# Attention stage of a hybrid kernel: the fronts of all four sequences moved ahead of the attention loop, split parts of all eight units kept in DRAM, rotary halves swapped by DMA

## The reference

```python
cq  = gelu(x @ wq + bq)            # 64 latent channels
q_c = cq @ wqc + bqc               # 128 "content" channels
q_r = x @ wqr + bqr                # 128 "rotary" channels
ckv = gelu(x @ wkv + bkv); k_c = ckv @ wkc + bkc; k_r = x @ wkr + bkr
v   = (ckv @ wv + bv)              # 16 heads of 16
q_r, k_r = rope(q_r), rope(k_r)    # t * cos + concat(-t2, t1) * sin
q, k = gelu(concat(q_c, q_r)), gelu(concat(k_c, k_r))   # exact in float32
out = softmax(causal(q k^T / 4)) v
x   = x + (out @ wo + bo)          # x was layer-normed at the input of q, k, v
```

## Time and profile before

| | |
|---|---|
| runs | 5124.07, 5140.43, 5151.45 us; median 5140.43 |
| the profiled execution | 5133.93 us, its span 5132.2 us |
| attention stage in it | from about 3717 to 4726 us |
| ahead of its loop | 3717 to 3854 us |
| the loop | 3854 to about 4718 us, then the last output products |
| mean granted PE clock | 0.867 of 2.4 GHz |

### The profile page before, as it was taken

One profiled execution on the slowest core, in us unless ns is written; L12 is line 12 of the kernel. 1 busy time (PEld: TensorE's weight loads), 2 busy tenths in 40 slices (PEclk: granted clock), 3 DMA queues, 4 the chain that ended last, 5 costly groups with the idle time before them and its releaser, 6 DMA issues.

```text
span 5132.2 us, 49428 instructions
## 1 busy us (share of the span) xinstructions
PE 3978.6 (78%) x15218; PEld 2283.6 (44%) x15218; DVE 2808.6 (55%) x4916; ACT 2304.2 (45%) x4166; POOL 2539.4 (49%) x2184
## 2 busy tenths in 40 slices
PE   6888878769948777996778699948937777788892
PEld 2333333357715455773333356645712323233571
DVE  6999999841156663114888822255244545454422
ACT  5566656321157663113555333332525555555241
POOL 6999999722222333114889644423552424222256
PEclk8999999869969887997888799969957878889896
DMA  5666666512110001223555411150532404221145
GB/s 151 160 156 161 161 160 155 149 42 96 64 50 17 33 25 57 82 78 103 150 153 144 137 43 45 45 158 20 149 87 52 79 19 70 38 39 39 51 130 133
DMA packets 310841, 472.53 MB, mean 92 GB/s; under 512 B 34634, under 2 KB 167734, under 8 KB 310506
## 3 DMA queue, kind: packets, MB, share of 16 engines
q1 hardware_dynamic: 277152, 388.87, 28.9%
q0 software_dynamic: 29184, 76.12, 5.3%
q10 hardware_dynamic: 4224, 4.19, 0.2%
HBM read 375.26 MB, written 97.49 MB: 92 GB/s over the span
## 4 chain that ended last, share of the span: by engine, by line
PE 39%; DVE 6%; POOL 6%; ACT 5%; issue 5%; DMA 3%; SPq 0%; another core or an unknown queue 0%; DVEq 0%; POOLq 0%; ACTq 0%
PE s_gate_up L2305 7%; PE s_result_sum L2321 4%; PE s_out_sum L3632 3%; PE s_hidden_sum L1745 3%; PE s_result_sum L1756 3%; PE s_scores_T L3616 2%; POOL s_h L435 2%; PE s_shared L2961 2%; DVE s_maxima L3272 2%; PE s_scores L3577 2%; PE s_shared L2971 1%; PE s_transposed L2295 1%; POOL s_gathered L1047 1%; POOL s_h L444 1%; DMA s_bc<-s_bc_rows 1%
## 5 line engine op out<-in xcount | busy, mean ns | idle before, releaser
L435 POOL TENSOR_TENSOR s_h<-s_dtu,s_bc 128x1024 f32<-128x1024 f32 x384 | 904.2, 2363 | 73.0 <-PE s_y_sum L477 54.1
L477 PE MATMUL s_y_sum<-s_h,identity 128*128 128x512 f32 x1536 | 770.3, 639 | 160.5 <-POOL s_h L444 151.5
L402 ACT ACTIVATE s_decay<-s_dt,s_A 128x512 f32<-128x512 f32 x768 | 498.4, 682 | 330.3 <-DVE s_h L377 323.3
L477 PEld LDWEIGHTS s_y_sum<-s_h,identity 128*128 128x128 f32 x1536 | 295.0, 202 | 599.2 <-issue 302.4
L3430 ACT ACTIVATE s_weights_T<-s_scores_T 128x1024 f32<-128x1024 f32 (+3 forms) x384 | 302.9, 810 | 369.9 <-PE s_scores_T L3616 364.7
L3272 DVE TENSOR_REDUCE s_maxima<-s_scores 128x1 f32<-128x512 f32 (+3 forms) x438 | 279.0, 659 | 318.0 <-PE s_scores L3580 223.3
L2305 PE MATMUL s_gate_up<-s_w_gate_up,s_rowsT 128*128 x1184 | 420.8, 488 | 3.2 <-issue 2.5
L444 POOL TENSOR_TENSOR s_h<-s_h,s_bc 128x512 f32<-128x512 f32 x288 | 367.0, 1275 | 23.4 <-DVE s_h L370 15.5
L2364 DVE TENSOR_TENSOR s_mid<-s_act,s_gate_up 128x128 f32<-128x128 f32 (+1 forms) x228 | 92.9, 408 | 455.4 <-ACT s_act L2337 433.1
L3492 POOL TENSOR_SCALAR_AFFINE_SELECT s_weights_T<-s_weights_T 128x256 f32<-128x256 f32 x256 | 104.3, 412 | 458.6 <-ACT s_weights_T L3430 457.3
L370 DVE TENSOR_TENSOR_SCAN s_decay<-s_decay,s_carry,s_h 128x512 f32<-128x512 f32 x240 | 303.4, 1278 | 24.3 <-POOL s_clip_flag L2633 13.9
(11 more groups left out here) (525 smaller groups left out, 7989.9 us busy)
## 6 DMA issues: line engine op xcount, KB each, us to landing
s_bc<-s_bc_rows SPq DMA_DIRECT2D x384, 512.0 KB, 4.9
sorted_results<-s_result SPq DMA_DIRECT2D x160, 128.0 KB
s_w_inter<-in_L_ffn_experts_inter SPq DMA_DIRECT2D x16, 1024.0 KB
s_w_exp_out<-in_L_ffn_experts_out SPq DMA_DIRECT2D x16, 1024.0 KB
s_queries<-parts_of_q SPq DMA_DIRECT2D x96, 128.0 KB
s_keys<-parts_of_k SPq DMA_DIRECT2D x96, 128.0 KB
results_by_token<-zeros SPq DMA_DIRECT2D x16, 512.0 KB, 6.1
s_pair<-results_by_token SPq DMA_DIRECT2D x16, 512.0 KB, 6.8
```

Source lines behind the costliest of these rows:

```text
L402: S.e.activation(self.decay[:, (2 * g + d) % 4, :], dt[q // self.passes % 2][:, at, :], ACT.Exp, scale=A[:, at, g % ns:g % ns + 1]).then_i ...
L435: G.e.tensor_tensor(self.h[r][:], dtu[q // self.passes % 2][:, at:at + 2, :], mid(self.bc[r][:, 0, :], 2), ALU.mult).then_inc(*self.fed.up())
L477: made = T.e.matmul(self.y[:, d, :], ident[:], self.h[r][:, d, :], start=False, stop=g % ns == ns - 1)
```

## The change

1. A new function `head` runs ahead of the loop, for every engine, the combine, the front and the split of **all four** sequences as a pipeline with a period of 21 ticks for each sequence, and in it unit 0's maxima and values. `program` now starts at unit 0 and has only `project`, `bias`, `values`, `highest` and `maxima` as sides.
2. `stage` writes the parts of each unit to its own place in DRAM (8 units x 3 parts for q and for k), through a ring of three SBUF tiles. In the head SP stacks units 0 and 1; in the loop it stacks only.
3. The rotary halves are swapped by two DMAs issued by ACT; cos, sin and the sum move from POOL to DVE. Content and rotary tiles have SBUF of their own.
4. A split has two ACT casts (three before) and two subtractions, the second of which writes the third bf16 part. The rotary q tile is subtracted on DVE, the other three on POOL.
5. The combine's ring has four tiles (two before). The front's SBUF is shared with the loop's weights, outputs and the like; DVE and ACT wait at the loop's start until the last three parts tiles have been written to DRAM (`head_is_over`). All eight PSUM banks serve the head. `latent` is kept for each sequence.
6. Ticks of the loop: `FIRST` 14 to 10, `OUT` respaced.

```diff
-    combine = Combine(K, M, X, 2, 1)
+    combine = Combine(K, H, X, 4, 1)
+    parts = [H.sb(f"parts{i}", [P, 3, L], BF16) for i in range(3)]
+    dram = [K.nc.dram_tensor(f"parts_of_{n}", [NB * DT, 3, P, L], BF16, kind="Internal").ap() for n in "qk"]
+    PERIOD, HEAD_MAX, HEAD_VALUES = 21, 62, (112, 114)
+    GATHER, SUM, STATS, FACTORS = (-4, -2, 0, 2, 5, 8, 10, 12), (4, 6, 8, 9, 11, 13, 15, 18), (10, 19), (13, 20)
+    NORM, TURN, TURNED = ((14, 15), (21, 22)), ((16, 17), (24, 25)), ((17, 18), (25, 26))
+    LATENT, LATENT_MADE, CONTENT, CONTENT_MADE = (20, 31), (21, 32), ((23, 24), (34, 35)), ((25, 26), (35, 36))
+    ROTATE, ROTATED, CROSS, ROTARY_MADE = ((28, 30), (36, 38)), ((29, 31), (37, 39)), (35, 43), (39, 47)
+    SPLIT = (((36, 38, 40, 42), (38, 40, 42, 45)), ((41, 44, 45, 49), (48, 50, 52, 54)))
-    FIRST = 14
+    FIRST = 10
+    def head(**side):
+        work = [("setup", 0)]
+        for b in range(NB):
+            work += [(n, b) for n in ("gathers", "sums", "stats", "factors", "norm", "turn", "turned_rows", "latents",
+                                      "content", "rotate", "cross", "rotary")]
+            work += [("split", (b, ct, j)) for ct in range(DT) for j in range(2)]
+        work += [("highest", (0, 0)), ("maxima", (0, 0, False)), ("maxima", (0, 1, False)), ("values", 0)]
     def program(main, **side):
-        for u in range(-3, n_units + 1):
+        for u in range(n_units + 1):
-            if 0 <= u + 2 < n_units:
-                work += [("front", u + 2), ("split", (u + 2, 0)), ("split", (u + 2, 1))]
...
+        def stage(b, ct, j):
+            i = 4 * b + 2 * ct + j
+            Q.wait_ge(*split_done[ct][j].at(b))
+            Q.wait_ge(*staged[i % 3].at(i // 3 - 1))
+            Q.e.dma_start(dram[j][DT * b + ct].rearrange("a c t -> c a t"), parts[i % 3][:]).then_inc(*staged[i % 3].dma())
+        for b in range(NB):
+            if b == NB - 1:
+                stack_max(0, 0)
+            for ct in range(DT):
+                for j in range(2):
+                    stage(b, ct, j)
+                if b == 0:
+                    for a in range(2):
+                        stack(ct, a)
+        for u in range(n_units):
+            if 0 < u < n_units - 1:
+                stack(u + 1, 1)
+            stack_max(u, 1)
+            if u + 2 < n_units:
+                stack(u + 2, 0)
+            if u + 1 < n_units:
+                stack_max(u + 1, 0)
...
+    def rests(E, v):
+        b, ct, j = v
+        to = parts[(4 * b + 2 * ct + j) % 3]
+        yield PERIOD * b + SPLIT[ct][j][1]
+        E.wait_ge(*cast0[ct][j].at(b))
+        E.e.tensor_tensor(act[ct][j][:], act[ct][j][:], to[:, 0, :], ALU.subtract).then_inc(*rest[ct][j].up())
+        yield PERIOD * b + SPLIT[ct][j][3]
+        E.wait_ge(*cast1[ct][j].at(b))
+        E.e.tensor_tensor(to[:, 2, :], act[ct][j][:], to[:, 1, :], ALU.subtract).then_inc(*split_done[ct][j].up())
+    def head_is_over(E):
+        for i in range(2 * n_units - 3, 2 * n_units):
+            E.wait_ge(*staged[i % 3].at(i // 3))
...
+        def cross(b):
+            for j in range(2):
+                yield PERIOD * b + CROSS[j]
+                V.wait_ge(*swapped.at(2 * b + j))
+                for i, (to, table) in enumerate(((act[1][j], cos), (crossed, sin))):
+                    V.e.tensor_tensor(to[:], to[:], table[:], ALU.mult).then_inc(*v_step.up())
+                V.e.tensor_tensor(act[1][j][:], act[1][j][:], crossed[:], ALU.add).then_inc(*rope_added.up())
...
+                for half in range(2):
+                    S.e.dma_start(crossed[half * DC:(half + 1) * DC, :],
+                                  act[1][j][(1 - half) * DC:(2 - half) * DC, :]).then_inc(*swapped.dma())
-                for half in range(2):
-                    made = S.e.activation(crossed[half * DC:(half + 1) * DC, :],
-                                          straight[(1 - half) * DC:(2 - half) * DC, :], ACT.Copy)
```

More of the change, by code:

```diff
@@ L3112, in projects @@
         return range(u // DT * PAIRS - 2, u // DT * PAIRS) if u > 0 else ()
[L3114 to L3117 removed]
     B = Banks()
[L3120 removed]
+    B.of["bv"], B.of["max", 0, 0] = 7, 4
+    for i in range(2):
+        B.of["values", 0, i] = 3 + i
+    for a, n in ((0, PER), (1, EARLY)):
+        for i in range(n):
+            B.of["scores", 0, a, i] = 1 + i % 2
+    for u in range(n_units + 1):
@@ L3320, in main @@
                 beside(2 * s + 1)
-        program(main, setup=setup, combine=sums, front=front, maxima=maxima, highest=highest, project=project)
+        head(setup=setup, sums=sums, stats=stats, cross=cross, split=split, maxima=maxima, highest=highest)
+        head_is_over(V)
+        program(main, maxima=maxima, highest=highest, project=project)
+    def rests(E, v):
+        b, ct, j = v
+        to = parts[(4 * b + 2 * ct + j) % 3]
[8 more added lines that the diff above has]
+            E.wait_ge(*staged[i % 3].at(i // 3))
     def scalar():
@@ L3332, in setup, with norm @@
             made.then_inc(*bv_here.up())
+        def norm(b):
+            for i, c in enumerate(range(b * CPB, (b + 1) * CPB)):
+                for t in range(0, TPC, 2):
+                    yield PERIOD * b + NORM[i][t // 2]
+                    if t == 0:
+                        S.wait_ge(*ln.made.at(c))
+                        S.wait_ge(*turned.at(DT * c - 1))
+                    for a in (t, t + 1):
+                        made = S.e.activation(xn[:, a, :], X[:, TPC * c + a, :], ACT.Identity,
+                                              bias=ln.addend[:, 0, a:a + 1], scale=ln.factor[:, 0, a:a + 1])
+                made.then_inc(*ln.used.up())
@@ L3493, in main, with take @@
                 beside(2 * s + 1)
-        program(main, combine=sums, front=front, rope=rope, split=split, bias=bias)
+        head(gathers=gathers, factors=factors, split=split)
+        program(main, bias=bias)
     def tensor():
         T.wait_ge(*prepared.at(0))
-        free = [turned.at(-1)] * 3
-        ob_free = [turned.at(-1)]
-        def take(name, until):
-            f = B.of[name]
+        free = [turned.at(-1)] * len(bank)
+        def take(f, until):
             T.wait_ge(*free[f])
@@ L3660, in main @@
                     product(n - 2)
-        program(main, setup=setup, values=values, front=front, rotate=rotate, maxima=maxima, highest=highest, project=project)
+        head(setup=setup, turn=turn, latents=latents, content=content, rotate=rotate, maxima=maxima, highest=highest,
+             values=values)
+        program(main, values=values, maxima=maxima, highest=highest, project=project)
     sync()
```

440 lines of the change are left out of this document (199 added, 241 removed).

## The result

The kernel after takes 5057.44 us (median of 4 runs, 5052.76 to 5065.05) against 5135.31 us for the kernel before: a ratio of 0.9847, 95% interval 0.9816 to 0.9879. It is 78 us faster. The forecast was 4937 us, 198 us faster, with a range that ended at 5050. The direction was right; the size was less than half, and both terms of the sum were off by about the same 60 us.

A forecast was written before the change was run, and what follows sets the result against it. No engine was full, so the prediction counted only the attention stage, its loop units lengthened by fronts: 5133.9 - 256 (loop) + 59 (longer head) = 4937 us. The forecast went from 4890 to 5000, the range from 4860 to 5050.

The forecast's parts named there:

- Part 1: Loop: without fronts, units 0 to 6 fall from 114.6 to 78 us, a gain of 256 us (bounds 172 and 312).
- At full clock its 74.0 us of PE work at 0.88 would be 65, and with the same 12 us of idle time the unit would last 77: Loop: unit 6 before, which had no front, scaled to full clock to give the length of every unit.
- the window of 86.3 us: Loop before: last group of unit 5 to last of unit 6, taken as holding all of a unit without a front.
- the forecast's 78: Loop: length in us assumed for each unit from 0 to 6 without fronts, between 70 and 90.
- the rival of units of 90 us: Loop: stack copies come late, units last 90 us, total 5021 us; chance 0.10.
- the rival of the clock: Loop: the clock stays at 1.2 GHz, units last 126 us, total 5273 us, slower; chance 0.03.
- Part 2: Head: it grows, so the loop starts at 3913, 59 us later than before (bounds 25 and 125).
- Up to the gathers of the fourth sequence POOL runs in its written order, and I take it as the bound: Head: POOL's gathers, subtractions and norm factors set the pace, with the last gather ending at 3845.
- Staging behind stacking: Head: stagings queue behind stack copies on SP and hold ACT's casts and POOL's subtractions; 10 us (0 to 24).
- beside it: Head's tail of 48 us: unit 0's maxima, values and highest run alongside, costing up to 20 us if cover is short.
- Contention of POOL and DVE: Head: DVE operations with two SBUF inputs and POOL's tensor operations wait for each other; 10 us on POOL (0 to 60).
- The rival in which DVE's 70 us stand in series with POOL's work: Head: the shared port sets the pace, total 4997 us; chance 0.12.

The follow-up runs named there:

- b1_nostack: The kernel after without the stacking copies of units 2 to 7, which then use queries and keys of units 0 and 1; ratio 0.985 to the kernel before.
- a4_noprod: The kernel after with the output projection (turning the rows, product, addition into the residual) left out; units of 79.4 us, ratio 0.973 to the kernel before.
- a3_both: The kernel after with each tile's statistics halves together on DVE and units 0 and 1 stacked behind all four stagings of their sequence; 5016.36 us, ratio 0.978.
- d2_shrunk: a3_both with unit 0's score maxima in the head taken over the first 32 keys only, without mask there; head 209.8 us, ratio 0.977.
- c1_copies: The kernel after with the rotary halves swapped by two ACT copies, as in the kernel before, instead of two DMAs; ratio 0.983 to the kernel before.

## Why the prediction was right and wrong

**Right.** The seat of the time: fronts out of the loop raise its clock (0.84 to 0.92) and take PE, ACT and POOL work from it. The last 58 us stayed. No table load is left in the loop: ACT loads the exponential's table once, at 3971.53. The stack copies in the loop cost nothing (b1_nostack). The loop does not stay at 1.2 GHz.

**Part 1, 256 us forecast, 196 measured.** The step that failed is "At full clock its 74.0 us of PE work at 0.88 would be 65, and with the same 12 us of idle time the unit would last 77". No unit runs at full clock. By the windows above the clock is 0.94 in unit 1 and 0.89 in unit 5, and PE's busy time follows it: 72.44 x 0.94 = 68.1 and 76.87 x 0.89 = 68.4, with 14 us of idle time in both. So scaling by the clock was sound; the clock put in was not: the one window of the earlier trace rows that has a unit's products and values stood at 0.88. In the mean of units 1 to 6 PE is busy for 74.15 us at 0.92 and idle for 14.3. Of the 11.5 us between this unit of 88.5 and the 77, about 6 are the clock (74 against 68), 3 are work (68 against 65), and 2 idle time. Of the work 1.2 us are eight small products of the values: a unit from 1 to 5 has 486 matmuls, while the window of 86.3 us, which was said to have "all of it", has 478. The rest of the 3 us was not traced. The bare 86.3 us, which stood in the earlier trace rows, would have been the better number.

Over the forecast's 78, six units of 88.5 us are 63 us too long, and unit 0, which has no output product, lies some 3 below it: that is the 60. The output products are not what was left out. Every unit from 1 on carries two, but so did unit 6 of before, from which the 77 was taken. That a4_noprod comes out at 79.4, beside the forecast's 78, is luck: it lacks 9.1 us of work and waits that the forecast had in it. The rival of units of 90 us had the length nearly right and the reason wrong, since the stack copies cost nothing; the rival of the clock had the reason, but far too much of it. Each unit still has a stretch at low clock, as unit 6 had before: in unit 2 it lies between 4144 and 4160, at 0.68. Such stretches did not go with the fronts, and what brings them is not shown.

**Part 2, 59 us forecast, 118 measured.** The step that failed is "Up to the gathers of the fourth sequence POOL runs in its written order, and I take it as the bound". The pace was set by order. Measured from the stage's first load, the forecast head was 195.6 us (3913 - 3717.4) and the real one 254.5, beyond the 250 at which the prediction called itself wrong. Of these 59 us, 31.5 went with the two edits of order (a3_both): DVE's aggregation behind the rotary products of the sequence before, which the forecast did not have, and SP's stacks ahead of stagings ("Staging behind stacking", priced at 10). Another 13.2 went with unit 0's maxima (d2_shrunk), which the forecast had "beside it", at up to 20 us if the cover is short; it was short. What is left, 14.2 us, splits at the last gather: it comes in d2_shrunk at 138.3 instead of 127.6 us, and from there to the loop are 71.5 instead of 68 us. The cause of those 11 us at the gathers is not shown. DVE's additions wait 37.3 us for gathers to land, in 15 waits, where it was 13.6 us before, while stagings and stacks keep the DMA share at 0.98 for 60 us; no run took the DMA traffic out of the head, so this stays an argument.

**Contention of POOL and DVE** was priced at 10 us on POOL. Groups by line of the kernel after in the head, POOL's subtractions and the DVE operations that meet them:

```profile
L1064 DVE SCALAR_TENSOR_TENSOR residual<-s_gathered,pick_weight,residual 128x256 f32<-128x256 f32 x64 | 37.5, 586 | 38.5 <-DMA s_gathered<-sorted_results,pick_row 37.3
...
L3368 POOL TENSOR_TENSOR s_act1k<-s_act1k,s_parts 128x1024 f32<-128x1024 f32 x4 | 9.5, 2386 | 14.1 <-ACT s_parts L3452 14.1
...
L3371 DVE TENSOR_TENSOR s_parts<-s_act1q,s_parts 128x1024 bf16<-128x1024 f32 x4 | 6.8, 1692 | 3.9 <-ACT s_parts L3455 3.9
```

The 24 subtractions of POOL took 55 us, 4 more than 24 times 2.13. On DVE the additions took 586 ns in the mean instead of 490 undisturbed, 6 us in all: four of the 64, each beside a subtraction of POOL, took 1.5 to 3.0 us, and the others 0.45 to 0.52. The four subtractions took 1692 ns in the mean instead of 1210, all of it in one that met POOL's and took 3.11 us. The lock of the earlier trace rows is there, and costs some 4 us on POOL and 11 on DVE; how much of it lies on the way to the loop was not tested. The rival in which DVE's 70 us stand in series with POOL's work did not come. The Trainium skill (SBUF — State Buffer, Who interferes with whom) calls it an exclusive lock, and says that a DVE instruction with two SBUF inputs contends with a GpSimd instruction that reads SBUF. The trace agrees for tensor operations by the durations above, and shows next to none of it for gathers, which last 1045 ns here beside the additions and 1018 before.

## What to carry to other kernels

In a software pipeline whose order is written out by tick, a generator that yields between its parts can put a short instruction, on which the next stage hangs, behind another stage's wait; look in the profile for the waits upstream of the idle engine, not for the busiest engine. Two such chains side by side hide each other: one edit gained 14.7 us, the other 1.0, both 31.5, so an edit that does nothing alone is worth keeping until its neighbour is cut. And price a stretch of work by the whole length of a measured stretch with the same contents; if it is scaled to another clock, let it be a clock that such a stretch has had, not the full one.

## What the runs showed of the hardware that was not expected

In the head's last 20 us PE is busy for 15.35 us and still has a granted clock of 0.50, its low level of 1.2 GHz (the last row of the windows in the section on the result); in the 20 us before them it was busy for less, 10.97 us, and had 0.84. So unit 0's last maxima run at 1.2 GHz. The level comes back early in the loop, but not at one place. Windows of the kernel after and of c1_copies from the first loop matmul, 5 us, 5 us and 10 us:

```profile
3970.40:3975.40 5.00, 4.66 (x14) 1.70 (x13) 3.09 (x6) 3.86 (x4) 0.83 (x2) 0.50 0.02 3
3975.40:3980.40 5.00, 5.00 (x31) 2.61 (x30) 3.12 (x6) 2.56 (x5) 1.88 (x5) 0.74 0.00 0
3980.40:3990.40 10.00, 7.71 (x58) 3.68 (x57) 5.04 (x9) 4.50 (x7) 5.48 (x6) 1.00 0.00 0
```

```profile
3965.10:3970.10 5.00, 4.66 (x14) 1.65 (x13) 3.10 (x6) 3.78 (x4) 0.82 (x2) 0.50 0.01 3
3970.10:3975.10 5.00, 5.00 (x22) 1.79 (x20) 3.29 (x6) 2.25 (x4) 1.63 (x4) 0.50 0.00 0
3975.10:3985.10 10.00, 7.97 (x41) 3.83 (x38) 2.67 (x4) 2.77 (x5) 5.71 (x6) 0.67 0.00 0
```

The first 5 us are alike and the second are not: the clock has risen in one and not in the other, and the first group ends 28.0 or 33.0 us behind the first matmul. Eight of the thirteen kernels in the table show about 28 (27.6 to 28.3), four about 33 (32.8 or 33.0). d2_shrunk took 35.3: its clock, too, was 0.50 for the first 10 us, and ACT still waited 5.4 us for the last staging; 8 of its 13 us went there. What decides between 28 and 33 was not found out. It is as large as several of the edits above, so they are judged by more than one column. Within the loop it is the same: units with the same 486 matmuls and the same 14 us of idle time last from 85.5 us (a3_both, unit 4, clock 0.96) to 90.9 (unit 5 of the kernel after, 0.89), by the clock alone.
